# The first token tile of an output projection multiplied at the end of the scan before it, and its weights' halves made there

## The reference, cut to what matters

```
b, L, _ = hidden_states.shape                      # 4, 256, 512; D_IN = 1024, N = 16
...
def step(state, inp):
    dt_t, B_t, C_t, u_t = inp
    dA = jnp.exp(dt_t[..., None] * A)
    state = state * dA + (dt_t * u_t)[..., None] * B_t[:, None, :]
    y = jnp.einsum('bdn,bn->bd', state, C_t)
    return (state, y)
...
_, ys = jax.lax.scan(step, init, xs)
y = ys.transpose(1, 0, 2) + x * D
y = y * jax.nn.silu(gate)
return y @ W_out.T
...
x = x + _layernorm(_L0_attn_ref(_layernorm(x, axis=-1), ...), axis=-1)
x = x + _layernorm(_L0_ffn_ref(_layernorm(x, axis=-1), ...), axis=-1)
```

## Time and profile before

| | us |
|---|---|
| median of 3 runs (1718.52 to 1719.4) | 1718.96 |
| the profiled execution | 1724.65 |
| its span in the trace | 1722.9 |
| last batch of the scan, from its first recurrence to its last | 425.4 to 507.0 |
| end of the scan, barrier and start of "fa" up to PE's first product | 507.0 to 518.1 |
| "fa", from PE's first product to its last | 518.1 to 585.3 |

### The profile page before, as it was taken

The page is one execution under the profiler, slowest core; times in us unless marked ns, Lnnn a source line. Parts: engine busy times, 40 slices in busy tenths (PEclk is TensorE's granted clock), DMA queues, the critical chain, the costliest instruction groups (busy, mean ns, idle before and its releaser), DMA issues. The chain is left out here.

```text
span 1722.9 us, 25631 instructions
## 1 busy us (share of the span) xinstructions
PE 1615.5 (94%) x8758; PEld 1380.3 (80%) x8758; DVE 1111.2 (64%) x1588; ACT 895.2 (52%) x1905; POOL 767.4 (45%) x442
## 2 busy tenths in 40 slices
PE   5996899999988999899989999999999998899998
PEld 3862799999977778677868988989898987788776
DVE  4336999999986343364717777677767677665422
ACT  2336888888764354235426454555555554443221
POOL 2211799999975274244411221222313223555343
PEclk9998899999999999999999999999999998999999
DMA  3201001001102393002100010001100102144100
GB/s 120 67 1 58 1 7 49 30 27 52 53 12 87 145 349 128 19 1 86 44 25 25 26 50 24 24 24 35 38 24 24 52 34 74 59 162 147 37 19 31
DMA packets 25195, 97.79 MB, mean 57 GB/s; under 512 B 3104, under 2 KB 3360, under 8 KB 22688
## 3 DMA queue, kind: packets, MB, share of 16 engines
q1 hardware_dynamic: 24976, 96.75, 15.8%
q10 hardware_dynamic: 144, 0.07, 0.0%
HBM read 94.57 MB, written 2.23 MB: 56 GB/s over the span
## 5 line engine op out<-in xcount | busy, mean ns | idle before, releaser
L872 POOL TENSOR_TENSOR scratch_s<-scratch_s,scan_cm 128x1024 f32<-128x1024 f32 x96 | 227.3, 2368 | 26.4 <-DVE scratch_s L1044 26.1
L1868 POOL TENSOR_TENSOR stretch_turned<-stretch_turned,res_const 128x1024 f32<-128x1024 f32 x32 | 77.1, 2410 | 293.2 <-ACT stretch_turned L1711 293.2
L1556 PE MATMUL psum<-opnd_xh,query_wqh 128*128 128x256 f32 x512 | 150.2, 293 | 1.9 <-PEq L94 1.9
L1138 PE MATMUL psum<-res_const,scratch_s 128*128 128x128 f32 x1088 | 144.7, 273 | 2.2 <-POOL scratch_s L872 2.2
L1556 PE MATMUL psum<-opnd_xl,query_wqh 128*128 128x256 f32 x512 | 144.8, 283 | 0.0
L1556 PE MATMUL psum<-opnd_xh,query_wql 128*128 128x256 f32 x512 | 144.8, 283 | 0.0
L1138 PEld LDWEIGHTS psum<-res_const,scratch_s 128*128 128x128 f32 x1088 | 128.7, 141 | 18.4 <-POOL scratch_s L872 2.4
L1719 ACT ACTIVATE stretch_pa<-psum,stretch_nm 128x128 f32<-128x128 f32 x128 | 45.2, 365 | 158.8 <-DVE stretch_nm L1966 158.8
L1132 PE MATMUL psum<-scan_diag,scratch_s 128*128 128x256 f32 x448 | 112.6, 388 | 6.7 <-ACT scratch_s L920 6.7
L928 ACT ACTIVATE scratch_s<-ssm_dt,ssm_vec 128x255 f32 (+1 forms) x256 | 112.4, 501 | 8.6 <-DVE scratch_s L1044 5.9
L1132 PE MATMUL psum<-diag_odd_diag,scratch_s 128*128 128x256 f32 x448 | 110.0, 380 | 0.0
(11 more groups left out here) (332 smaller groups left out, 4725.2 us busy)
## 6 DMA issues: line engine op xcount, KB each, us to landing
mi_dw<-in_dw SPq DMA_DIRECT2D x24, 448.0 KB, 5.5
mi_dm<-in_dm SPq DMA_DIRECT2D x24, 448.0 KB, 6.2
query_raw<-in_w_q SPq DMA_DIRECT2D x8, 1024.0 KB, 4.8
query_raw<-in_w_o SPq DMA_DIRECT2D x8, 1024.0 KB, 4.7
gu_raw<-in_w_gu SPq DMA_DIRECT2D x11, 512.0 KB, 5.9
mlpa_raw<-in_w_mlp SPq DMA_DIRECT2D x7, 768.0 KB, 4.4
mlpa_base<-in_b_mlp SPq DMA_DIRECT2D x7, 768.0 KB, 5.8
mlpb_raw<-in_w_mlp SPq DMA_DIRECT2D x7, 768.0 KB, 4.3
```

The costliest lines, as they stand in the source:

```text
L872: nc.gpsimd.tensor_tensor(slot[h][r], slot[h][r], weights(4 * h, 4), ALU.mult).then_inc(weighted_pool, 1)
L1138: mm = nc.tensor.matmul(ps_y[:, t * P:(t + 1) * P], part[:, t * P:(t + 1) * P], ident, start=start and t == 0, stop=stop and t == QT - 1, ...
L1556: mm = nc.tensor.matmul(ps_q[:, h * SEQ:(h + 1) * SEQ], w[:, k, h * HD:(h + 1) * HD], x[:, k, b * SEQ:(b + 1) * SEQ], start=(k == 0 and w ...
L1868: nc.gpsimd.tensor_tensor(heads(turned[:, :]), heads(turned[:, :]), over_heads(C_SIN, SEQ), ALU.mult).then_inc(q_sine, 1)
```

## The change

The output weights are loaded in the middle of the last batch but one. In the last batch ACT makes one high part of the weights behind each tile's skip product (`out_weight`), and behind the last tile the high part of token tile 1. PE multiplies token tile 0 with the weights as they are, in plain fp32, 8 products in place of 24 (`first_product`): three ahead of the last `slot_sums`, one ahead of the last `back`, four behind it. DVE waits for POOL's last product, then makes the eight low parts of the weights in the place of the weights themselves, each after PE's product with it, and the low part of token tile 1. "fa" begins with the products of tile 1, and with the layer norm of tile 0.

```diff
--- before
+++ after
@@ finish_phase @@
+        hh_of = lambda t: hh[t % 2] if begun is None or t != 1 else begun[0]
+        hl_of = lambda t: hl[t % 2] if begun is None or t != 1 else begun[1]
+    made, split = (0, 0) if begun is None else (1, 2)
...
             def step(t, s):
-                if proj and t == 0 and halves is not None:
+                if t < made:
+                    pass
+                elif proj and t == 0 and halves is not None:
...
-                    at_least(pe, h_hi, t + 1)
-                    at_least(pe, h_lo, t + 1)
+                    at_least(pe, h_hi, t + 1 - split)
+                    at_least(pe, h_lo, t + 1 - split)
...
-            if proj and halves is not None:
+            if split:
+                hidden_hi(2, 0)
+            elif proj and halves is not None:
...
-                at_least(pool, y_ready, t - 1)
-                at_least(pool, h_hi, t + 1)
+                at_least(pool, y_ready, t - 1 - made)
+                at_least(pool, h_hi, t + 1 - split)
...
-                    at_least(dve, y_ready, t + 1)
+                    at_least(dve, y_ready, t + 1 - made)
@@ scan_phase, SP @@
             for b in range(1, BATCH):
                 load(b)
-            sp.wait_ge(scanned, (BATCH - 1) * KI * (PAIRS + 1))
-            sp.wait_ge(u_ready, (BATCH - 1) * KI + 1)
-            sp.dma_start(w_next[:, :, :], w_next_dram).then_inc(w_in, 16)
+                if b == BATCH - 2:
+                    sp.wait_ge(scanned, (b * KI + KI // 2) * (PAIRS + 1))
+                    sp.wait_ge(u_ready, b * KI + KI // 2 + 1)
+                    sp.dma_start(w_next[:, :, :], w_next_dram).then_inc(w_in, 16)
@@ scan_phase, ACT @@
+            def out_weight(j, r):
+                act.wait_ge(w_in, 16)
...
+                nc.scalar.activation(out, src, ACT.Copy).then_inc(out_hi, 1)
...
                     if b < BATCH - 1:
                         diagonals(b + 1, j * 2 + r)
+                    else:
+                        out_weight(j, r)
...
             pairs(act, body)
+            act.wait_ge(gated, KI)
+            nc.scalar.activation(out_hidden[0][:, :, :], token_tile(1), ACT.Copy).then_inc(token_hi, 1)
             keep(TILES - 1)
             finish(TILES - 1)
@@ scan_phase, DVE @@
             pairs(dve, body)
+            dve.wait_ge(weighted_pool, TILES * SLOTS)
+            for k in range(KI):
+                dve.wait_ge(out_hi, k + 1)
+                dve.wait_ge(out_multiplied, k + 1)
+                nc.vector.tensor_tensor(out_wl[k], w_next[:, k, :], f32(out_wh[k]), ALU.subtract).then_inc(out_lo, 1)
+            dve.wait_ge(token_hi, 1)
+            nc.vector.tensor_tensor(out_hidden[1][:, :, :], token_tile(1), f32(out_hidden[0][:, :, :]), ALU.subtract).then_inc(token_lo, 1)
+            dve.wait_ge(token_lo, 1)
+            dve.wait_ge(out_lo, KI)
@@ scan_phase, PE @@
+            def first_product(k):
+                nc.tensor.matmul(ps_out, token_tile(0)[:, k, :], w_next[:, k, :], start=(k == 0), stop=(k == KI - 1)).then_inc(out_multiplied, 1)
             pairs(pe, body)
             own_sums(TILES - 1, 1)
+            pe.wait_ge(scanned, scans_by(TILES - 1, -1))
+            pe.wait_ge(gated, KI)
+            pe.wait_ge(w_in, 16)
+            for k in range(3):
+                first_product(k)
             slot_sums(TILES - 1, 1, 2)
+            first_product(3)
             back(TILES - 1)
+            for k in range(4, KI):
+                first_product(k)
@@ program @@
+    out_high = at("out_high", 80)("wh", [P, KI - 2, DM], F32R), at("out_high_end", 132)("wh", [P, 2, DM], F32R)
+    out_low = at("out_low", 116)("wl", [P, KI, DM], F32R)
...
-                 hidden=tile_of(x_conv), w_raw=w_res,
+                 hidden=tile_of(x_conv), halves=out_halves, begun=out_hidden,
```

More of the change, by code:

```diff
@@ L160, in finish_phase @@
 def finish_phase(nc, tag, M, place, K, hidden=None, gate=None, w_raw=None, acc=None,
-                 out_scale=None, last_out=None, norm_only=False, ahead=(), x_loads=(), halves=None, next_split=(), next_products=()):
+                 out_scale=None, last_out=None, norm_only=False, ahead=(), x_loads=(), halves=None, begun=None, next_split=(), next_products=()):
     signals = Signals(nc)
@@ L278, in hidden_hi @@
             def hidden_hi(t, s):
-                at_least(act, y_ready, t - 1)
+                at_least(act, y_ready, t - 1 - made)
                 src = hidden(t, s)
@@ L302, in step @@
             def step(t, s):
-                if proj and t + 1 < TT:
+                if proj and (split + 1 if split else 0) <= t + 1 < TT:
                     hidden_hi(t + 1, 1 - s)
@@ L355, in step @@
                     gating(t + 3, 1 - s)
-            if proj:
+            if proj and not split:
                 gating(0, 0)
@@ L724, in widen_phase, with scan_phase @@
     signals.close()
-def scan_phase(nc, M, place, par, x_conv, gate, dt, bc_dram, bm, cm, b_turned, diag, more_decay, w_next, w_next_dram, wx, wdt, block_mean):
+def scan_phase(nc, M, place, par, x_conv, gate, dt, bc_dram, bm, cm, b_turned, diag, more_decay, w_next, w_next_dram, out_high, out_wl, out_hidden, wx, wdt, block_mean):
     signals = Signals(nc)
@@ L742, in scan_phase @@
     w_in = sem("next_weight_in")
+    out_hi, out_lo, token_hi, token_lo = sem("out_weight_hi"), sem("out_weight_lo"), sem("token_hi"), sem("token_lo")
+    out_multiplied = sem("out_multiplied")
+    EARLY_OUT = KI - 2
+    out_early, out_late = out_high
+    out_wh = [out_early[:, k, :] for k in range(EARLY_OUT)] + [out_late[:, k, :] for k in range(KI - EARLY_OUT)]
+    token_tile = lambda t: x_conv[:, t // QT, :].rearrange("p (d c) -> p d c", d=KI)[:, :, (t % QT) * P:(t % QT + 1) * P]
+    ps_out = M.ps[:, 1, :]
     b_in, c_in = sem("b_in"), [sem(f"c_in{h}") for h in range(SLOTS)]
@@ L947, in diagonals @@
                     ins.then_inc(diag_made, 1)
+            def out_weight(j, r):
+                act.wait_ge(w_in, 16)
+                if isinstance(j, int):
+                    src, out = w_next[:, j * 2 + r, :], out_late[:, r, :]
+                else:
+                    src, out = [w[:, bass.ds(j * 2 + r, 1), :].rearrange("p a c -> p (a c)") for w in (w_next, out_early)]
+                nc.scalar.activation(out, src, ACT.Copy).then_inc(out_hi, 1)
             def body(b, j, switch):
```

15 lines of the change are left out of this document (9 added, 6 removed).

## The result

The changed kernel takes 1714.54 us, the median of 11 runs (1712.1 to 1717.53). The kernel before, over 11 runs beside them, has 1720.42. The ratio is 0.9966 with a 95% interval of 0.9959 to 0.9974, so the change saves 5.8 us (4.5 to 7.1). A later set of runs of the same kernel (after_again) gave 0.9963 (0.9949 to 0.9977). The forecast was a gain of 5.7 us and a time of 1713.3, in a range of 1710.5 to 1715.8. The time came out 1.2 us higher than forecast although the gain agrees, because the kernel before has a median of 1720.42 over 11 runs, where the forecast started from 1718.96 over three. One run of the kernel before, beside the first experiments, took 3786.47 us, a slow run that the ratios leave out. The profiled execution took 1715.53 us with a span of 1713.7.

The account below looks back on a forecast made before the run. PE, busy 94% of the span, gains only where it waits or sheds work. Tile 1 starts 7.1 us earlier, low clock loses 1.6, tile 3 starts 5.7 earlier: 1718.96 - 5.7 = 1713.3 us, range 1710.5 to 1715.8.

Parts of the forecast that it names:

- The load and ACT's copies: Scan's last two batches: load costs nothing, eight copies of 0.53 us hidden in ACT's idle time; otherwise 4.2 us.
- The unsplit products: Scan's end: eight plain fp32 products of 0.86 us, 6.9 us in all, starting at 507.26, results at 515.6.
- DVE as the end of the phase: Scan's end: DVE replaces gating as last, following PE's 0.86 pace, subtractions done at 516.3, tokens' low part at 517.5.
- The border: Between scan phase and projection: 1.20 us, so "fa" starts at 518.7, 4.8 us later than before.
- The clock: Projection's tile 1: 3.3 us PE gap brings 3.4 us of low clock, a loss of 1.6 us; bounds 0 and 2.8.
- stays high in the gap: Rival at PE's gap before "fa": clock does not fall, 1.6 us more won, 1711.7; chance 0.17.
- What is late next: Projection: tile 2 does not wait; tile 3 waits for its low part, starting at 532.6, 5.7 us earlier.
- the low end's reserve: Projection: the shorter chain of an emptier POOL could win another 1 us, giving the low end of 1710.5.
- gives some of it back: Rival in the projection: new DVE and POOL collisions on two odd tiles cost 2 x 1.6 us; 1716.5, chance 0.12.
- the slower one: Rival at the scan's end: clock falls before the unsplit products, 1.71 us each; 2.6 us slower, 1721.6, chance 0.03.
- One sign: Profile after the change: eight recurrence groups a tile at the old pace, with the scan's end at 507.
- My sum: Tile 1's start 7.1 us earlier: 11.9 taken away (4.2 split waiting, 7.7 tile 0) against a 4.8 later start.

Follow-up runs that it names:

- copies_twice: Changed kernel with each of ACT's eight weight copies in the scan's last batch made twice, the first into unread memory; ratio to the kernel before 0.9961.
- products_behind: Changed kernel with all eight unsplit products placed behind the last sums and last turn; ratio to the kernel before 0.9983.
- warm_two: Changed kernel plus two filler fp32 products on PE behind the eight, into an unread bank; ratio to the kernel before 0.9950.
- token_first: Changed kernel with DVE making tile 1's token low part ahead of the weights' low parts; ratio to the kernel before 0.9955.
- tile1_high: Changed kernel with tile 1's eight high-by-high products moved ahead of the border, behind the unsplit ones; ratio to the kernel before 0.9952.
- token_first_high: Changed kernel with DVE making tile 1's low part first and four of tile 1's high-by-high products ahead of the border; 1711.19 us, ratio to before 0.9942.
- warm_gap: Changed kernel plus four filler fp32 products on PE behind the eight, into an unread bank; ratio to the kernel before 0.9958.
- The two half experiments: Against the kernel before: splits made in the scan for tile 0 without unsplit products, 1.0004; unsplit products and early load with splits left in the projection, 0.9993.

## Why the prediction was right, step by step

Counted from the last recurrence's end (my times less 507.0, as for the earlier trace rows):

| step | predicted | measured |
|---|---|---|
| PE's last turn starts | 4.8 | 4.41 |
| results of the last unsplit product | 8.6 | 8.23 |
| DVE's last subtraction ends | 10.5 | 10.16 |
| PE's first product of "fa" | 11.7 | 11.46 |
| low clock on tile 1 | 3.4 | 3.4 |
| tile 2 starts, without a wait | 18.8 | 18.61 |
| tile 3 starts | 25.6 | 25.17 |
| tile 3, gain against before | 5.7 | 6.13 |

**The load and ACT's copies** cost nothing, as forecast; copies_twice showed the slack. (A copy in the scan took 0.62 us instead of 0.53.) From the end of the products behind the second idle stretch of the scan phase (L1220, L1258 after the change; see the end) to the last recurrence the kernel before takes 352.4 us and the changed one 352.3. The forecast had DVE set the pace of that batch, from its 81.32 busy us of 81.60; PE's records fill the batch too, and no experiment here tells which of the two does.

**The unsplit products** took 0.86 us each. The term that was mis-sized, by 0.3 us, is where they start: I let them begin at the end of the last sum's record (0.27 behind the last recurrence), but matmul records overlap, and they began at 0.10; the same tail was counted again ahead of the sums and of product 3. The Trainium skill (FP8 and Floating Point Precision, TensorE Precision Notes) gives true fp32 four passes through the array. The traces come near it: a product of 512 columns at the full clock takes 0.86 us against 0.227 for an fp32r one, 3.8 times as long. So the eight unsplit products are not less work for PE than the 24 split ones: they take 6.9 us, and 24 times 0.227 is 5.4. They pay because they stand where PE was idle, and because they need no split ahead of them.

**DVE as the end of the phase.** Right, and the pace by PE too (products_behind). The gating met a subtraction: two of them took 1.55 us at 510.27 instead of 1.3. This was hidden, since the next waits for PE.

**The border** was 1.27 us, I had 1.20 from POOL's end.

**The clock** was the least certain term. It was low for 3.4 us, the value taken, and warm_two priced it at 1.56 us (1.6 forecast). That the figure was met exactly is in part luck: the clock fell only behind tile 1's third product here, and in after_again it fell before the tile, so that 2.65 us of it lay on tile 1. The rival "stays high in the gap" did not happen in any of the four traces with a gap of 3.24 us; with 2.17 us and less it did (token_first, warm_two, tile1_high, token_first_high and warm_gap, one trace each).

**What is late next.** Tile 3, at 25.17, with a wait of 0.52 us, as said ("under 1 us"). The chain from tile 1's result to it was 0.2 to 0.3 us shorter than the 6.7 I took over from the kernel before, because POOL had no other power waiting ahead of it; this was named as the low end's reserve. From tile 3 on the gain grew from 6.13 to 6.35 at the MLP's first product. Of the rivals, "gives some of it back" did not happen, nor did the slower one: the granted clock was 1.00 throughout the unsplit products. One sign did not come: the scan ended at 504.5 and not at 507, for a reason that lies ahead of the change (see the end).

**The range** has a slip at its high end. The case "gives some of it back" was to cost 3.2 us (2 x 1.6), and half of that would have been added; I added half of 2.5, which was the gain left. By its own terms the high end is 1716.1 and not 1715.8. The measured 1714.54 lies inside both.

By the trace the change is thus worth 6.35 us, 0.65 more than predicted, of which 0.24 come from the earlier start; by the runs it is worth 5.8 (4.5 to 7.1). The runs can't tell these two figures apart.

What I had not seen is how the gain divides. My sum booked 4.2 us for the splits' wait and 7.7 for tile 0 against 4.8 of later start, as if the items were independent. The two half experiments show that they are not: alone they give 0.43 and 1.71 us.

## What to carry to other kernels

Moving preparation ahead of a phase border gains nothing by itself if the border then waits for it; it needs another engine's work to hide behind, and that work is best taken from the next phase. At a border ask which engine arrives last: put what it could do during its waits in front (2.7 us here for one reordered subtraction), and fill the other engines' idle time only up to that point, not into the border itself. After a short idle stretch PE's clock is a term of the sum: one gap of 3.2 us cost 1.6 us behind it. The reordering and the clock are priced here by single traces; the intervals of these variants' runs overlap that of the changed kernel.

## What the runs showed of the hardware that was not expected

Early in the scan phase, far ahead of the change and in code that is the same in all these kernels, PE idles twice for 2.8 us. In some executions the clock falls after the first, the second or both, in others not. PE alone, granted clock behind the busy time, of the kernel before, the changed one and tile1_high:

```profile
121.98:127.00 5.02, 5.02 (x8) 0.66 0.00 0
146.90:154.00 7.10, 6.17 (x8) 0.52 0.51 92
```
```profile
122.60:127.00 4.40, 4.34 (x11) 1.00 0.00 0
146.90:154.00 7.10, 7.10 (x19) 0.76 0.37 110
```
```profile
121.98:127.00 5.02, 4.62 (x11) 1.00 0.00 0
146.90:154.00 7.10, 7.10 (x24) 1.00 0.36 104
```

The last recurrence then ends at 507.0, 504.5 and 502.3 us. All twelve traces agree with this. The products that PE makes behind the first idle stretch take 10.5 or 8.8 us, those behind the second 6.7, 5.4 or 3.7, and the last recurrence ends at 506.4 to 507.0 where both are longest and at 502.3 to 502.6 where both are shortest. From the end of these last products to the last recurrence it is 352.1 to 352.4 us in every one of them. So 4.7 us of difference between spans have nothing to do with what was changed, as much as most of these experiments move, which is why spans of single executions mislead here and a stretch counted from a fixed instruction does not. That these draws make up the scatter of the run times (1718.52 to 1724.49 for the kernel before) is likely, but only the profiled executions show a clock, so it is not shown.
